# Mixture logits kept slots-on-partitions in a three-block decoder layer on one NeuronCore

## The reference

```python
xn, se = rms_norm(x, gamma_x), rms_norm(slot_embeds, gamma_slot)
logits = einsum('bsd,etd->bset', xn, se)            # 256 tokens x 1024 slots for each sequence
dispatch = softmax(logits, axis=1)                  # over the tokens
slots = einsum('bsd,bset->betd', xn, dispatch)
h = gelu(slots @ w1)                                # 256 -> 1024
processed = h @ w2                                  # 1024 -> 256
combine = softmax(logits.reshape(b, s, e * t), axis=-1)   # over the 1024 slots
out = einsum('bnd,bsn->bsd', processed, combine)
```

## Time and profile before

| what | value |
|---|---|
| median of 3 runs | 1773.68 us (1773.43 to 1777.49) |
| span of the profiled execution | 1770.5 us |
| around the span, to the median | 3.2 us |
| busy: PE, PEld, DVE, ACT, POOL | 1735.7, 1570.7, 1158.1, 1018.4, 439.5 us |
| granted TensorE clock, mean | 0.999 of 2.4 GHz |
| one turn of the loop | 105.4 us |

### The profile page before, as it was taken

One profiled execution on the slowest core, in us unless ns is written; L12 is line 12 of the kernel. 1 busy time (PEld: TensorE's weight loads), 2 busy tenths in 40 slices (PEclk: granted clock), 3 DMA queues, 4 the chain that ended last, 5 costly groups with the idle time before them and its releaser, 6 DMA issues.

```text
span 1770.5 us, 40859 instructions
## 1 busy us (share of the span) xinstructions
PE 1735.7 (98%) x17306; PEld 1570.7 (89%) x17306; DVE 1158.1 (65%) x2307; ACT 1018.4 (58%) x1775; POOL 439.5 (25%) x354
## 2 busy tenths in 40 slices
...
DMA packets 20852, 19.67 MB, mean 11 GB/s; under 512 B 9920, under 2 KB 19776, under 8 KB 20288
## 3 DMA queue, kind: packets, MB, share of 16 engines
...
## 4 chain that ended last, share of the span: by engine, by line
PE 85%; ACT 5%; DVE 4%; issue 4%; POOL 1%; DMA 0%; POOLq 0%; SPq 0%; DVEq 0%; ACTq 0%
PE ps L465 21%; PE ps L466 19%; PE ps L467 19%; PE ps L590 3%; PE ps L573 2%; PE ps L553 2%; PE ps L775 2%; PE ps L700 2%; PE ps L620 2%; PE ps L843 2%; PE ps L665 1%; PE ps L766 1%; POOL h_lo L1446 1%; PE ps L872 1%; ACT L1034 1%
## 5 line engine op out<-in xcount | busy, mean ns | idle before, releaser
L1446 POOL TENSOR_TENSOR h_lo<-h_f,h_hi 128x512 fp32r<-128x512 f32 x256 | 336.9, 1324 | 1052.7 <-DVE h_hi L1329 1052.7
L465 PE MATMUL ps<-sl_hi,w_hi 128*128 128x256 f32 x1024 | 304.9, 298 | 5.4 <-DVE sl_lo L1088 2.9
L465 PE MATMUL ps<-w_hi,h_hi 128*128 128x256 f32 x1024 | 300.9, 294 | 5.5 <-POOL h_lo L1446 5.3
L466 PE MATMUL ps<-w_hi,h_lo 128*128 128x256 f32 x1024 | 290.1, 283 | 0.0
L467 PE MATMUL ps<-w_lo,h_hi 128*128 128x256 f32 x1024 | 289.8, 283 | 0.0
L466 PE MATMUL ps<-sl_hi,w_lo 128*128 128x256 f32 x1024 | 288.8, 282 | 0.0
L467 PE MATMUL ps<-sl_lo,w_hi 128*128 128x256 f32 x1024 | 288.8, 282 | 0.0
L465 PEld LDWEIGHTS ps<-sl_hi,w_hi 128*128 128x128 f32 x1024 | 194.4, 190 | 28.9 <-ACT h_f L1034 14.2
L1329 DVE CAST h_hi<-h_f 128x512 fp32r<-128x512 f32 x256 | 175.4, 691 | 67.1 <-ACT h_f L1034 66.3
L1034 ACT ACTIVATE h_f<-ps 128x512 f32<-128x512 f32 x256 | 151.2, 598 | 104.6 <-PE ps L467 103.6
L465 PEld LDWEIGHTS ps<-w_hi,h_hi 128*128 128x128 f32 x1024 | 196.0, 191 | 15.0 <-POOL h_lo L1446 11.3
...
## 6 DMA issues: line engine op xcount, KB each, us to landing
...
```

The lines of the kernel that those rows point to most:

```text
L465: te.matmul(o, lhs[0], rhs[0], start=first, stop=False)
L466: te.matmul(o, lhs[1], rhs[0], start=False, stop=False)
L1446: Q_.tensor_tensor(h_lo[:, part, :], h_f[:, part, :], h_hi[:, part, :].bitcast(f32), ALU.subtract)\
```

## The change

The logits are computed with slots on partitions from the start: the slot embeddings are the stationary operand and the 256 tokens the moving one, so a batch takes 48 matmuls of 256 columns where it took 24 of 512. `lt` and `comb` go, and `cm` and `ed` read the logits from SBUF. What was a reduction along the row for the maximum over slots is now one across partitions: `rx` (DVE) takes the maximum over the 8 slots that a partition holds, for each of 256 tokens, reading `lg` with a stride of 1 KB; `rxt` (PE) transposes its 256 columns in two pieces; `rm` (DVE) reduces them from PSUM; `rmb` (PE) brings the negated maxima back along the row, in two more transposes of a broadcast column; `rb` (ACT) copies them to SBUF. `ar` (DVE) adds them to a chunk of logits, `cb` on ACT then takes the exponential twice, once rounded to fp32r and once in f32, and `cb` on POOL makes the lo part that DVE made before. The sums over the slots are made by `sum` (DVE, seven additions of 256 columns a batch) and `rs` (PE, two f32 matmuls against a column of ones). `rxt`, `rmb` and `rs` are users of bank 0. The tables START, ORDER and FINISH are new throughout; START has 150 idle matmuls where it had 197. The loads by DMA and their order are the same.

```diff
 ORDER = dict(
     pe="""
-        m.lt.0 l.outer.3.0 d.kv m.dispatch.0 l.outer.3.1 c.xt.1 m.slots.0 l.comb.3 d.xt.2 c.k c.q d.q2 c.v
-        m.hidden.0.0 d.scores2.0 m.hidden.0.1 m.hidden.0.2 d.mt2.0 m.hidden.0.3 m.lt.1 l.combine.3 d.shifted2.0
...
+        d.kv l.outer.3.0 m.dispatch.0 l.outer.3.1 m.rxt c.xt.1 m.slots.0 m.rmb c.k d.xt.2 c.q c.v d.q2 m.hidden.0.0
+        d.scores2.0 m.hidden.0.1 m.hidden.0.2 d.mt2.0 m.hidden.0.3 l.combine.3 l.rs d.shifted2.0 m.outer.0.0
...
 START = dict(
...
     act="""
-        c0.xt.1 s0.hi.0 s0.hi.1 c0.k c0.q c0.kh c0.qh s0.hi.2 c0.mh.0 c0.ex.0 s0.se_squares c0.xo.0 c0.mh.1 c0.ex.1
...
+        s0.hi.0 s0.hi.1 s0.hi.2 c0.xt.1 c0.k c0.q c0.kh c0.qh s0.se_squares c0.mh.0 c0.ex.0 c0.xo.0 c0.mh.1 c0.ex.1
...
-        lg = at("lg", [P, NT, SLOTS], f32, r_lg)
+        lg = at("lg", [P, NC, 2, S], f32, r_lg)
...
             def logits(a, k):
...
-                t, u = divmod(k, 2)
-                for dk in range(ND):
-                    last = three(ps[:, 1 + k, :], both(XD, full, dk, slice(t * P, t * P + P)),
-                                 both(W["se"], full, dk, slice(u * 512, u * 512 + 512)), dk == 0, dk == ND - 1)
+                for e in range(2):
+                    slot = slice(k * CHUNK + e * P, k * CHUNK + (e + 1) * P)
+                    for dk in range(ND):
+                        last = three(ps[:, 1 + k, e * S:(e + 1) * S], both(W["se"], full, dk, slot),
+                                     both(XD, full, dk), dk == 0, dk == ND - 1)
                 last.then_inc(s["lg_ps"], 1)
 
 
-            def lt(b, c):
-
-                if c == 0:
-                    pe.wait_ge(s["lg_sb"], nth("lg_sb", b, 4))
-                    if not later(b):
-                        pe.wait_ge(s["k_ev"], nth("k_ev", 1, 1))
-                    if later(b):
-                        pe.wait_ge(s["ge"], nth("ge", b - 1, 15))
...
+            def rxt(b):
+
+                misc_free("m.rxt", b)
+                pe.wait_ge(s["rx"], nth("rx", b, 1))
+                for t in range(NT):
+                    last = te.transpose(ps[:, 0, t * P:(t + 1) * P], xh_d[:, 0, t * P:(t + 1) * P], ident[:, :])
+                last.then_inc(s["rxt_ps"], 1)
+
+            def rmb_step(b):
+
+                misc_free("m.rmb", b)
+                pe.wait_ge(s["rm"], nth("rm", b, 1))
+                for t in range(NT):
+                    last = te.transpose(ps[:, 0, t * P:(t + 1) * P], rm[:, t:t + 1].broadcast_to([P, P]), ident[:, :])
+                last.then_inc(s["rmb_ps"], 1)
+
+            def rs(b):
+
+                misc_free("m.rs", b)
+                pe.wait_ge(s["sm"], nth("sm", b, 7))
+                for t in range(NT):
+                    last = te.matmul(ps[:, 0, t:t + 1], total[:, t * P:(t + 1) * P], ones_f[:, 0:1], start=True, stop=True)
+                last.then_inc(s["rs_ps"], 1)
+
+            def dispatch(b, c):
+
+                pe.wait_ge(s["edn"], nth("edn", b, c + 1))
+                if c == 0 and later(b):
+                    pe.wait_ge(s["ge"], nth("ge", b - 1, 15))
+                elif c == 0:
+                    pe.wait_ge(s["k_ev"], nth("k_ev", 1, 1))
...
-            def comb(b, c):
...
-                for e in range(2):
-                    for t in range(NT):
-                        last = te.transpose(ps[:, comb_bank(b), e * S + t * P:e * S + (t + 1) * P],
-                                            ecomb[:, t, e * P:(e + 1) * P], ident[:, :])
-                last.then_inc(s["cb_ps"], 1)
...
             def ed(b, c):
...
-                    last = nc.scalar.activation(edt[:, e, :], ps[:, 6, e * S:(e + 1) * S], ACT.Exp,
+                    last = nc.scalar.activation(edt[:, e, :], lg[:, c, e, :], ACT.Exp,
...
-            def ec(b, c):
...
-                for t in range(NT):
-                    last = nc.scalar.activation(ecomb[:, t, :], lg[:, t, c * CHUNK:(c + 1) * CHUNK], ACT.Exp,
-                                                bias=rm[:, t:t + 1], accum_out=rsum[:, t, c:c + 1])
-                last.then_inc(s["ec"], 1)
...
+            def rb(b):
+
+                act.wait_ge(s["rmb_ps"], nth("rmb_ps", b, 1))
+                if later(b):
+                    act.wait_ge(s["ar"], nth("ar", b - 1, NC))
+                copy(rmb[:, :], ps[:, 0, 0:S]).then_inc(s["rmb"], 1)
 
             def cb(b, c):
-                act.wait_ge(s["cb_ps"], nth("cb_ps", b, c + 1))
+                act.wait_ge(s["ar"], nth("ar", b, c + 1))
...
-                copy(comb_tile(b)[0][:, :, :], halves(comb_bank(b))).then_inc(s["cb_hi"], 1)
+                nc.scalar.activation(comb_tile(b)[0][:, :, :], ecomb[:, :, :], ACT.Exp)
+                nc.scalar.activation(ecomb[:, :, :], ecomb[:, :, :], ACT.Exp).then_inc(s["cb_hi"], 1)
...
-            def row_max(b):
-
+            def rx(b):
+
+                dve.wait_ge(s["xs_lo"], nth("xs_lo", b, 1))
                 dve.wait_ge(s["lg_sb"], nth("lg_sb", b, 4))
-                for t in range(NT):
-                    V.tensor_reduce(rm[:, t:t + 1], lg[:, t, :], AX, ALU.max, negate=True).then_inc(s["rm"], 1)
+                V.tensor_reduce(xh_d[:, 0, :], lg[:, :, :, :].rearrange("p c e s -> p s (c e)"), AX, ALU.max)\
+                    .then_inc(s["rx"], 1)
+
+            def rm_step(b):
+
+                dve.wait_ge(s["rxt_ps"], nth("rxt_ps", b, 1))
+                V.tensor_reduce(rm[:, :], ps[:, 0, 0:S].rearrange("p (t s) -> p t s", t=NT), AX, ALU.max, negate=True)\
+                    .then_inc(s["rm"], 1)
+
+            def ar(b, c):
+
+                if c == 0:
+                    dve.wait_ge(s["rmb"], nth("rmb", b, 1))
+                if c or later(b):
+                    dve.wait_ge(s["cb_lo"], nth("cb_lo", b, c))
+                    dve.wait_ge(s["sm"], nth("sm", b, max(0, 2 * c - 1)))
+                V.tensor_tensor(ecomb[:, :, :], lg[:, c, :, :], rmb[:, :].unsqueeze(1).broadcast_to([P, 2, S]), ALU.add)\
+                    .then_inc(s["ar"], 1)
+
+            def sum_step(b, c):
+
+                dve.wait_ge(s["cb_hi"], nth("cb_hi", b, c + 1))
+                if c == 0:
+                    if later(b):
+                        dve.wait_ge(s["rs_ps"], nth("rs_ps", b, 0))
+                    V.tensor_tensor(total[:, :], ecomb[:, 0, :], ecomb[:, 1, :], ALU.add).then_inc(s["sm"], 1)
+                    return
+                for e in range(2):
+                    dve.wait_ge(s["sm"], nth("sm", b, 2 * c - 1 + e))
+                    V.tensor_tensor(total[:, :], total[:, :], ecomb[:, e, :], ALU.add).then_inc(s["sm"], 1)
 
             def cm_step(b, c):
-                dve.wait_ge(s["lt_ps"], nth("lt_ps", b, c + 1))
-                V.tensor_reduce(cm[:, 2 * c:2 * c + 2], halves(6), AX, ALU.max, negate=True).then_inc(s["cm"], 1)
+                dve.wait_ge(s["lg_sb"], nth("lg_sb", b, c + 1))
+                V.tensor_reduce(cm[:, 2 * c:2 * c + 2], lg[:, c, :, :], AX, ALU.max, negate=True).then_inc(s["cm"], 1)
...
+            def cb(b, c):
+                pool.wait_ge(s["cb_hi"], nth("cb_hi", b, c + 1))
+                hi, low = comb_tile(b)
+                Q_.tensor_tensor(low[:, :, :], ecomb[:, :, :], hi[:, :, :].bitcast(f32), ALU.subtract).then_inc(s["cb_lo"], 1)
...
             def finish(b):
...
-                dve.wait_ge(s["ec"], nth("ec", b, NC))
-                V.tensor_reduce(rtot[:, :], rsum[:, :, :], AX, ALU.add).then_inc(s["rs_sum"], 1)
-                dve.wait_ge(s["rs_sum"], nth("rs_sum", b, 1))
-                V.reciprocal(rrec[:, :], rtot[:, :]).then_inc(s["rr"], 1)
+                dve.wait_ge(s["rs_ps"], nth("rs_ps", b, 1))
+                V.reciprocal(rrec[:, :], ps[:, 0, 0:NT]).then_inc(s["rr"], 1)
                 dve.wait_ge(s["rr"], nth("rr", b, 1))
...
```

More of the change, by code:

```diff
@@ L98 @@
[L98 to L102 removed]
+        s0.idle.10 s0.idle.2 c0.xt.1 s0.idle.6 c0.k c0.q c0.v s0.idle.8 s0.idle.8 c0.scores.0 s0.idle.7 s0.idle.4
@@ L150 @@
[L150 to L154 removed]
+        d-1.kv l-3.outer.3.0 m-2.rxt m-2.dispatch.0 m-2.rmb d-1.xt.2 m-2.slots.0 l-3.outer.3.1 m-2.hidden.0.0
```

330 lines of the change are left out of this document (147 added, 183 removed).

## The result

| | median us | span us | clock |
|---|---|---|---|
| before | 1775.3 (1773.4 to 1777.5) | 1770.5 | 0.999 |
| after | 1795.4 (1794.7 to 1801.6) | 1793.6 | 0.989 |

The account below looks back on a forecast made before the run. TensorE's list was taken as the bound. 15 batches at -1.2 us make -18, batch 0 gives 0, the start +5: -13 on the 1770.5 span is 1757.5, with 3.2 around it 1761 us; range 1738 to 1781.

Parts of the forecast that it names:

- TensorE's list: Loop: transposes dropped save 3.5 us a batch, new steps and longer logits cost 1.05; list shorter by 2.45.
- New waits: Loop, TensorE: waits of 0.74 from rxt to xt, 0.2 at rmb, 0.7 from ob to mt; 1.65 us a batch.
- The two adjacent pairs: Loop, TensorE: rxt directly before xt and ob directly before mt, each needing an evacuation; waits of 0.74 and 0.7 us.
- Old waits given back: Loop, TensorE: small earlier waits, mostly ahead of dispatch and behind moved steps, would go; 0.4 us a turn back.
- the rival in which the waits eat the gain: Loop: new waits pass 2.85 us a turn, leaving only the start; about 1773 us, 1769 to 1778; chance 0.18.
- `rx` at 2.3: Loop, DVE: the reduction over 2048 elements takes 2.3 us; the forecast is wrong if it is over 3.5.
- the rule that spoke against it: SBUF is read in 16-byte lines, so an f32 stride beyond 4 elements isn't free; supports the slow-rx rival, chance 0.10.
- The rival was priced by twice the row: Loop, DVE: rx at 4.6 us delays TensorE, 20 to 35 us in all; 1781 to 1796, say 1785; chance 0.10.
- The first stretch: Start: first projection at 16.5 instead of 11.99 (+4.5), slower clock +1.5, earlier dispatch -1; +5 us, of 0 to +9.
- fewer idle matmuls save nothing: Start, TensorE: 47 fewer idle matmuls save nothing, since the chain of one sequence sets the time.
- the rival with a start of over 12 us: Start: the new first stretch costs over 12 us; chance 0.05.
- DVE, ACT and POOL are no bound: Loop: DVE's turn goes from 72 to 75 us of 104; ACT and POOL have a third of the time or more spare.

Follow-up runs that it names:

- e4: The changed kernel with the token maxima taken by four element-wise instructions on contiguous rows instead of the strided reduction; 1780.6 us, 1.0042 of the kernel before.
- e2: The changed kernel with the mask and gammas later on DVE and the copies of wv and wq2 later on ACT; 1787.1 us, 1.0081 of the kernel before.
- e5: The changed kernel with the first stretch of the kernel before on all engines, up to the first logits; 1779.9 us, 1.0029 of the kernel before.

## Why the prediction was wrong, point by point

The span was forecast at 1757.5 and is 1793.6. Of the 36.1 between them 13.4 lie up to the second kv (+18.4 for +5), 12.9 in the 14 turns (-3.9 for -1.2 each) and 9.8 behind the last kv (+8.6 for -1.2).

- **TensorE's list, -2.45 a turn.** Measured -2.0, worked out as I had costed it, from the starts of TensorE's instructions in one turn: `comb` and `lt` took 1.75 and 1.50 before (3.25; I had 3.5), the logits went from 5.73 to 6.10 (+0.37; I had +0.2), `rs` takes 0.43 (0.44), `rmb` 0.19 (0.22), `rxt` 0.22 as forecast. Right in kind, a fifth too large. Busy time fell by 1.8 only, for one thing since the first 0.16 of every new wait lie under the end of the row ahead and count as busy.
- **New waits, 1.65 a turn.** Measured 1.84 as idle time, and 2.3 from start to start, as I had forecast them: `rxt` to `xt` 1.24 (0.74 forecast), `rxt` for the maxima 0.45 (none), `rmb` none (0.2), `ob` to `mt` 0.64 (0.7). The two adjacent pairs were the right places, and the price at `ob` was right. The excess at `xt` and `rxt` is `rx`: with the maxima of e4 the wait of `xt` is 0.5 idle, some 0.67 by starts, and that of `rxt` is gone.
- **Old waits given back, 0.4.** What is left of the turn's change of -0.28 after -2.0 and +2.3 is -0.6, so this was about right. Of the 0.9 by which the turn missed its -1.2, 0.4 are the list and 0.7 the new waits, less 0.2 here.
- **Two slips in the sums** changed nothing: 0.44, 0.44 and 0.2 are 1.08 and not 1.05; and the rival in which the waits eat the gain leaves the start alone, which with my own +5 is 1779 and not 1773.
- **`rx` at 2.3.** This step failed as such: 3.81, beyond the 3.5 that I had named as the point at which the forecast is wrong. I took the length from a row of the same size that read contiguous PSUM and gave the rule that spoke against it 0.10. At this place the 1.2 us by which it is longer than the maxima's 2.6 were worth 1.06 a turn (e4). The rival was priced by twice the row at +20 to +35; it alone made some 15 against the maxima (e4).
- **The first stretch, +5 of 0 to +9.** Measured +18.4 to the second kv, the largest miss. The projection was as said, 16.71 for 16.5, with wq_hi copied from 14.72 on (14.5), and the clock below 1 soon after. What failed is that I costed one moved step of ACT's table and did not follow the moved steps of DVE's: the mask ahead of k's shuffle waits for a transfer until 24.7, and the low part of wqk ahead of `xh_a` would have held the projection back to 13.7 without wq_hi too (e2). And the clock: I had written that fewer idle matmuls save nothing, not that they cost; at 76 to 90 the clock is 0.52. With the order of before on all engines 15.5 of the 18.4 come back (e5), so most of it is order and not work. The rival with a start of over 12 us had 0.05.
- **The end.** It had no term at all but its share of the turns. It was +8.6: about 1 of it half clock, 2 the strided reduction, and 5.5 open.
- **DVE, ACT and POOL are no bound.** DVE has 75.2 of 105.3 a turn, as forecast; it held for shares and not for the order of its list.

What decided is not one of my rivals but two of them together, rx and start, and a third place that I had not looked at.
